# Window attention with graph experts on one core: another order of the first stage's side tasks, in 8 slots per image

## The reference, cut to what matters

```python
x = x + _L0_conv_ref(_ln_c(x), w_qkv, b_qkv, w_o, b_o)     # two window attentions
t = _to_tokens(x)
t = t + _L0_ffn_ref(_ln_t(t), ...)                          # graph attention, top 2 of 4 experts
```

## Time and profile before

| what | value |
|---|---|
| median of 3 runs | 7772.78 us |
| the profiled execution: its time | 7765.42 us |
| its span, first to last instruction | 7763.3 us |
| stage `attention` in it | 0 to about 1878 us |
| busy in the whole span: PE, DVE, ACT, POOL | 50%, 63%, 28%, 67% |

### The profile page before, as it was taken

The page is one execution under the profiler, slowest core; times in us unless marked ns, Lnnn a source line. Parts: engine busy times, 40 slices in busy tenths (PEclk is TensorE's granted clock), DMA queues, the critical chain, the costliest instruction groups (busy, mean ns, idle before and its releaser), DMA issues. The chain is left out here.

```text
span 7763.3 us, 91006 instructions
## 1 busy us (share of the span) xinstructions
PE 3878.5 (50%) x32088; PEld 2504.7 (32%) x32088; DVE 4875.5 (63%) x6373; ACT 2140.9 (28%) x4331; POOL 5177.2 (67%) x5802
## 2 busy tenths in 40 slices
PE   5889999996334334333433333343334334333347
PEld 3667676664122212212221222122122212211123
DVE  9999999997455445545554554455455445545578
ACT  4779888884111111111111111111111111111000
POOL 4443444434777777777777777777777777777674
PEclk8999999997666666666666666666666666666578
DMA  1222222223112111111211111111112111111188
GB/s 51 54 58 63 63 61 66 64 55 73 33 34 44 33 33 39 38 33 33 45 33 33 39 38 33 33 43 35 33 33 44 33 33 39 38 33 33 34 258 278
DMA packets 504189, 417.71 MB, mean 54 GB/s; under 512 B 161058, under 2 KB 400850, under 8 KB 503378
## 3 DMA queue, kind: packets, MB, share of 16 engines
q1 hardware_dynamic: 322562, 340.11, 13.8%
q0 software_dynamic: 181344, 73.74, 9.4%
HBM read 203.44 MB, written 176.45 MB: 49 GB/s over the span
## 5 line engine op out<-in xcount | busy, mean ns | idle before, releaser
L1646 POOL DMA_INDIRECT edge_G<-node_rows,edge_src x4352 | 4127.2, 948 | 1326.3 <-issue 1326.3
L1701 PE MATMUL edge_hbank<-edge_xt,edge_w 128*128 128x512 f32 x1024 | 718.4, 858 | 2754.8 <-ACT edge_hid L1671 2740.6
L1450 DVE TENSOR_TENSOR edge_oh<-edge_wbank,edge_dlf 128x3072 bf16<-128x3072 f32 x512 | 1682.9, 3350 | 57.1 <-PE edge_cbank L1726 41.6
L1407 DVE COPY edge_O<-edge_O 128x24 f32<-128x24 f32 x64 | 12.3, 192 | 2349.4 <-DMA edge_G<-node_rows,edge_src 2349.4
L1701 PEld LDWEIGHTS edge_hbank<-edge_xt,edge_w 128*128 128x128 f32 x1024 | 253.6, 274 | 3184.0 <-ACT edge_hid L1671 3032.5
L1681 ACT ACTIVATE edge_w<-edge_w 128x272 f32<-128x272 f32 x64 | 27.5, 429 | 4048.4 <-DVE edge_w L1421 4048.4
L1726 PE MATMUL edge_cbank<-edge_oh 128*128 128x256 bf16 x4096 | 803.3, 366 | 650.2 <-DVE edge_oh L1450 649.8
L1726 PEld LDWEIGHTS edge_cbank<-edge_oh 128*128 128x128 bf16 x4096 | 476.9, 125 | 952.8 <-DVE edge_oh L1450 815.3
L599 POOL TENSOR_TENSOR attn_att<-attn_oraw,attn_rsum 128x512 f32<-128x512 f32 (+1 forms) x136 | 169.7, 1248 | 827.4 <-DVE attn_rsum L1143 735.1
L1070 DVE TENSOR_TENSOR attn_keys<-attn_keys 128x1024 f32<-128x1024 f32 (+1 forms) x340 | 480.2, 1412 | 9.8
L1075 DVE TENSOR_TENSOR attn_keys<-attn_keys 128x1024 f32<-128x1024 f32 (+1 forms) x340 | 481.3, 1416 | 0.0
(11 more groups left out here) (281 smaller groups left out, 6556.6 us busy)
## 6 DMA issues: line engine op xcount, KB each, us to landing
edge_G<-node_rows,edge_src POOLq DMA_INDIRECT x4352, 2.4
expert_out<-edge_yo SPq DMA_DIRECT2D x64, 1024.0 KB, 4.3
comb_ye<-expert_out SPq DMA_DIRECT2D x32, 2048.0 KB, 13.7
state_rows<-edge_O SPq DMA_DIRECT2D x64, 816.0 KB
attn_km<-attn_kT SPq DMA_DIRECT2D x1024, 32.0 KB, 2.0
attn_xin<-in_x SPq DMA_DIRECT2D x32, 512.0 KB, 4.3
attn_x<-in_x POOLq DMA_DIRECT2D x64, 256.0 KB, 4.8
x_rows<-attn_x SPq DMA_DIRECT2D x32, 512.0 KB, 3.3
```

Of the source, the lines that this page charges most:

```text
L1450: dve.tensor_tensor(oh[:, r:r + WIDE, :, :].rearrange("p t k n -> p (t k) n"), iota.unsqueeze(1).to_broadcast([P, 3 * WIDE, P]), dlf[:, t: ...
L1646: pool.indirect_dma_start(G[b][:, t, :], None, node_rows, bass.IndirectOffsetOnAxis(ap=src[b][:, t:t + 1], axis=0)).then_inc(s_g[b][2 * t ...
L1701: pe.matmul(hbank[k % 2][:, :], w1[:, k // HB, (k % HB) * P:(k % HB + 1) * P], xt[b][:, :], start=True, stop=True).then_inc(s_l1, 1)
```

## The change

Four pairs of tasks move, and the sort's table follows. `Ao1`, `Bo1` go from slot 3 to slot 4. `Ao0`, `Bo0` go from slot 7 to slot 0 of the next step (lags 0 and 2 become 1 and 3). `CZ0`, `CZ1` go from slot 5 to slot 6, with POOL's DMAs behind them; the statistics of x2 on DVE and `deviation(1)` on POOL go from slot 7 to slot 0 of the next step. `CH0` goes from slot 6 to slot 5, ahead of `Bk0`; `Bq0` stays in slot 6, now behind the CZ tasks. `Bv0` goes from slot 0 to slot 7 of the step before (lag 2 becomes 1), and its wait is written for the new place. SP stores the turned tokens before x2. The table in `spare` gets eight new numbers.

```diff
-        SLOT_TASKS = [["Av0", "Bv0"],
+        SLOT_TASKS = [["Av0", "Ao0", "Bo0"],
                       ["Ak1", "Bk1", "Aq1"],
                       ["Bq1", "Av1", "Bv1"],
-                      ["FT0", "FT1", "Ao1", "Bo1"],
-                      ["Ak0", "Aq0"],
-                      ["Bk0", "CZ0", "CZ1"],
-                      ["Bq0", "CH0"],
-                      ["CT0", "CT1", "Ao0", "Bo0"]]
-        LAG = {"Av0": 0, "Bv0": 2, ...
+                      ["FT0", "FT1"],
+                      ["Ak0", "Aq0", "Ao1", "Bo1"],
+                      ["CH0", "Bk0"],
+                      ["CZ0", "CZ1", "Bq0"],
+                      ["CT0", "CT1", "Bv0"]]
+        LAG = {"Av0": 0, "Bv0": 1, ...
...
-               "Bk0": 1, "Bq0": 1, "CZ0": 3, "CZ1": 3, "Ao0": 0, "Bo0": 2, ...
+               "Bk0": 1, "Bq0": 1, "CZ0": 3, "CZ1": 3, "Ao0": 1, "Bo0": 3, ...
...
-            busy += (0.85, -0.1, 0.05, 0.2, 3.05, -0.5, 0.55, 2.4)[j]
+            busy += (2.65, 0.4, 0.05, 0.8, 2.55, -0.2, 0.1, 0.1)[j]
...
# SP: the store of x2 (CZ0) now stands behind the store of the turned tokens (CT0)
...
# POOL
-                    if j == 5 and active("CZ0", n):
+                    if j == 6 and active("CZ0", n):
                         add_residual(n - LAG["CZ0"])
-                    if j == 7 and active("CZ0", n):
-                        deviation(1, n - LAG["CZ0"])
+                    if j == 0 and active("CZ0", n - 1):
+                        deviation(1, n - 1 - LAG["CZ0"])
...
# ACT, values()
-                    act.wait_ge(s_pv, (n - 1) * PAIRS + 4 * h + 4)
+                    act.wait_ge(s_pv, (m - 1 + LAG[task[0]]) * PAIRS + 4 * h + 4)
...
# DVE
-                    if j == 7 and active("CZ0", n):
-                        m = n - LAG["CZ0"]
+                    if j == 0 and active("CZ0", n - 1):
+                        m = n - 1 - LAG["CZ0"]
                         dve.wait_ge(s_added, 32 * m + 32)
                         statistics(1, x2, range(TILES), m)
```

More of the change, by code:

```diff
@@ L361, in attention @@
         s_store = sem("s_store")
-        SLOT_TASKS = [["Av0", "Bv0"],
+        SLOT_TASKS = [["Av0", "Ao0", "Bo0"],
                       ["Ak1", "Bk1", "Aq1"],
                       ["Bq1", "Av1", "Bv1"],
-                      ["FT0", "FT1", "Ao1", "Bo1"],
-                      ["Ak0", "Aq0"],
-                      ["Bk0", "CZ0", "CZ1"],
-                      ["Bq0", "CH0"],
-                      ["CT0", "CT1", "Ao0", "Bo0"]]
-        LAG = {"Av0": 0, "Bv0": 2, "Ak1": 0, "Bk1": 2, "Aq1": 0, "Bq1": 2, "Av1": 0, "Bv1": 2,
+                      ["FT0", "FT1"],
[3 more added lines that the diff above has]
+                      ["CT0", "CT1", "Bv0"]]
+        LAG = {"Av0": 0, "Bv0": 1, "Ak1": 0, "Bk1": 2, "Aq1": 0, "Bq1": 2, "Av1": 0, "Bv1": 2,
                "FT0": -1, "FT1": -1, "Ao1": 1, "Bo1": 3, "Ak0": -1, "Aq0": -1, "CH0": 5,
-               "Bk0": 1, "Bq0": 1, "CZ0": 3, "CZ1": 3, "Ao0": 0, "Bo0": 2, "CT0": 4, "CT1": 4, "A": 0, "B": 2}
+               "Bk0": 1, "Bq0": 1, "CZ0": 3, "CZ1": 3, "Ao0": 1, "Bo0": 3, "CT0": 4, "CT1": 4, "A": 0, "B": 2}
         FIRST_STEP, LAST_STEP = -2, IMAGES + 5
@@ L503, in _ @@
                     sp.dma_start(node_rows[m].rearrange("(j p) d -> p j d", p=P), hrow[:, :, :]).then_inc(s_hst, 16)
-                if active("CZ0", n):
-                    m = n - LAG["CZ0"]
-                    sp.wait_ge(s_added, 32 * m + 32)
-                    sp.dma_start(x2_out[m].rearrange("(j p) d -> p j d", p=P), x2[:, :, :]).then_inc(s_x2st, 16)
                 if active("CT0", n):
@@ L512, in _ @@
                     sp.dma_start(tnT_out[m], tnT[:, :]).then_inc(s_tst, 16)
+                if active("CZ0", n):
+                    m = n - LAG["CZ0"]
+                    sp.wait_ge(s_added, 32 * m + 32)
+                    sp.dma_start(x2_out[m].rearrange("(j p) d -> p j d", p=P), x2[:, :, :]).then_inc(s_x2st, 16)
             for late in sorted(transfers):
```

## The result

The changed kernel takes 7726.53 us, the median of 6 runs that lie between 7721.21 and 7733.56. Runs of the kernel before on the same chips have the median 7775.12 us (7772.62 to 7777.56, 6 runs). The ratio is 0.994, with a 95% interval of 0.993 to 0.9951: 48.6 us less by the medians, 38 to 54 us by the interval. The profiled execution took 7724.29 us with a span of 7722.2.

The account below looks back on a forecast made before the run. DVE was taken to bound stage `attention`, its work fixed, so only idle time could go. Terms -33 - 12 + 3 + 2 + 2 = -38 us took the median from 7772.8 to 7735, range 7710 to 7765.

Parts of the forecast that it names:

- What bounds the stage: Stage `attention`: DVE bounds it, 95.5% busy from step 10 to 31; only its idle time, 114 us there, can go.
- The wait for x2, -33: Slots 6 to 0: DMAs land at 7.2 us, statistics come at 11.2, so of 36.1 us of waits 3 stay.
- The rival that the wait only moves: DMAs behind the product start later and land behind the statistics; 32 us come back, total 7767; chance 0.13.
- Late transposes, -12: `Ao`, `Bo` come a slot after POOL's product, so PE's wait for POOL goes; -12 us, bounds 0 and -17.8.
- DVE felt it as part of the 17.8 us: PE's wait for POOL mostly cost nothing; DVE felt it within its L927 score waits behind slots 7 and 3.
- Slot 4 and slots without sort operations, +3 and +2: PE's 6.8 us in slot 4 just covered by its lead, +3; heavier slots without sort operations in steps 27, 31, +2.
- The drain, +2: After the last scores the last x2 statistics come a slot later, but queues are empty; +2 us, bounds 0 and 8.
- unchanged within 5 us: Profile sign: DVE's busy time to 1881 us stays the same within 5 us.
- DVE's work is fixed: Score passes, statistics and sort operations stay and are only spread by the planner, so only DVE's idle time can go.
- PE as the bound in slots 4 to 6: Rival: PE's lead missing in slot 4, DVE idles 2.4 us in 30 images, +72 - 3, total 7804; chance 0.07.
- The key copies: Rival: copies late for slot 4, 0.7 us per image back, total 7756, chance 0.04; PE waiting there a sign of error.
- That all waits go: Rival: evenly loaded PE also ends the L932 score waits except steps 27 and 31; -64, less 3, total 7712; chance 0.12.

Follow-up runs that it names:

- x2 half: Kernel before with only CZ tasks, `CH0`, POOL's DMAs, x2 statistics, `deviation(1)`, SP's order and 2.2 us of the table moved; 7736.76 us, 0.9944; again 0.9947.
- only the statistics late: Kernel before with only the x2 statistics, `deviation(1)` and 2.2 us of the table moved to slot 0 of the next step; 7760.31 us, 0.998.
- second profile of the changed kernel: The changed kernel run once more with no edit, against the kernel before on the same chip; 7723.56 us, 0.9937.
- the drain reordered: Changed kernel, last steps only: last two products ahead of image 30's `deviation(1)`, last statistics a slot earlier, ACT's normalisation of image 30 a slot later; 7724.96 us, 0.9941.
- the DMAs ahead of the product: Changed kernel with POOL issuing the two x2 DMAs ahead of slot 6's product by the row sums instead of behind it; 7735.71 us, 0.9951.
- coarse table: Changed kernel with the old numbers in `spare`, except 2.2 us for the statistics moved from slot 7 to slot 0; 7755.43 us, 0.9964 to the kernel before.
- fine table alone: Kernel before with only the new numbers in `spare`, the statistics' 2.2 us left in slot 7, all tasks where they were; 7787.21 us, 1.0005.
- attended half: Kernel before with only the attended tasks moved to slots 4 and 0 and `Bv0` to slot 7; 7776.65 against 7783.36 us, 0.9991.
- only the DMAs late: Kernel before with only POOL's x2 DMAs moved to slot 6 behind the product, CZ in slot 5, statistics in slot 7; 7854.07 against 7777.4 us, 1.0101.

## Why the prediction was right, point by point

**What bounds the stage.** Right: DVE. But the slots got shorter by two things where the prediction had one, by DVE's idle time (-42.8) and by its busy time (-12.3).

**The wait for x2, -33.** Measured -31.4 in the slots (34.4 to 3.0). The chain was worked out as 7.2 us for the landing against 11.2 for the statistics. The same step of the changed kernel:

```profile
969.29 0.34 DVE L1143 RECIPROCAL attn_rsum<-attn_oraw 128x32 f32<-128x32 f32 x1
969.78 1.06 POOL L599 TENSOR_TENSOR attn_att<-attn_oraw,attn_rsum 128x512 f32<-128x512 f32 x1 [0.35 <-DVE attn_rsum L1143]
970.78 2.69 POOL L583 DMA_DIRECT2D attn_x<-in_x  x2
980.34 1.58 DVE L1059 BATCH_NORM_STATS2 attn_st<-attn_x 128x6 f32<-128x128 f32 x8
```

The statistics come 11.05 us after the reciprocal. The issues end as forecast, but the landing takes longer:

```profile
DMA to landing us min/median/max: 4.4/5.7/8.0
```

The median is 5.7 us instead of 4.8. The second landing is then at about 970.78 + 1.35 + 5.7 = 977.8, and the margin is 2.5 us, not 4. With landings of up to 8.0 us it isn't enough everywhere: three waits are left, 1.8, 0.7 and 0.5 us, in steps 10, 11 and 19. The rival that the wait only moves was nearer than its 11.2 against 7.2 said, and the two kernels that leave the statistics in slot 7 behind late DMAs show it in full (127.3 and 110.4 us of waits).

**Late transposes, -12.** Measured 17.8 to 5.8 us under L927, exactly this, and in part by luck. It isn't the gain of moving the transposes: moved alone they gave 0.9991, and the x2 half, which leaves them where they were, got 8.0 of the 12.0 us, since its product was short again. The step "DVE felt it as part of the 17.8 us" was right as a row and incomplete as a cause, for more of the same lateness was hidden under the wait for x2, as the kernel with only the statistics late showed (32.9 us).

**Slot 4 and slots without sort operations, +3 and +2.** The waits under L932 for the scores of slot 5 went from 4.4 us in 7 to 6.1 in 7, so +1.7. Step 27 has 4.5 and 4.4 us of waits for the scores of slots 6 and 7 (8.9 where "some 7.5" was forecast, from terms that add up to 7.8; 4.51 before), step 31 4.1 for those of slots 3 and 4 instead of 5.8 for those of slots 2 and 3: +2.7 together. The sum under L932 is 0.7 up, as other steps lost some. The cover of PE's lead in slot 4 held with the new table and not with the coarse one.

**The drain, +2.** Measured +7.1, near the bound of 8, and +4.9 in the second profile of the changed kernel. "The queues are empty then and the data set the time" was wrong here. The last product of the kernel before, and then the drain of the changed kernel:

```profile
1843.95 1.41 POOL L599 TENSOR_TENSOR attn_att<-attn_oraw,attn_rsum 128x256 f32<-128x256 f32 x1 [1.39 <-DVE attn_rsum L1143]
```

```profile
1785.70 0.38 POOL L562 TENSOR_TENSOR attn_nw<-attn_st 128x8 f32<-128x8 f32 x1 [1.52 <-DVE attn_st L1059]
...
1792.20 0.24 DVE L1143 RECIPROCAL attn_rsum<-attn_oraw 128x16 f32<-128x16 f32 x1
...
1794.81 1.18 POOL L576 TENSOR_TENSOR attn_nw<-attn_nw 128x8 f32<-128x8 f32 x1
1795.96 1.59 POOL L599 TENSOR_TENSOR attn_att<-attn_oraw,attn_rsum 128x256 f32<-128x256 f32 x1
...
1797.70 1.09 PE L865 MATMUL attn_misc<-attn_ident,attn_att 128*128 128x128 f32 x4 [7.11 <-POOL attn_att L599]
...
1805.51 1.37 POOL L583 DMA_DIRECT2D attn_x<-in_x  x1 [7.95 <-ACT attn_x L696]
...
1821.85 0.20 POOL L576 TENSOR_TENSOR attn_nw<-attn_nw 128x8 f32<-128x8 f32 x1
```

The last reciprocal is there at 1792.20, but POOL is in `deviation(1)` of image 30 until 1796, and the last product starts 3.75 us after its reciprocal. In the kernel before POOL waited 1.39 us for this reciprocal and started 0.38 us after it, so the queue cost nothing. Followed along this chain, the 7.1 us are 0.4 to the reciprocal, 3.4 to the product, 1.8 from there to the issue of the last DMA, and 1.6 in its landing (1807.23 to 1814.73, against 5.9 us before); from the last statistics to `edges` both kernels take 19.3. The first three are -0.4, 3.4 and 1.6 in the second profile, and the landing 0.3, so the landing is mostly chance. The three sort operations that moved here are not on this chain. `deviation(1)` itself is slow: 10.3 us for image 30, with sort operations of 128x1024 beside its end, against 5.6 us for image 31; its last instruction takes 1.18 us there and 0.20 here. The kernel with the drain reordered takes the product ahead of it, and its drain is 2.7 to 4.9 us shorter.

**What the sum had not.** Shorter DVE operations, and three fewer in the slots. DVE is busy 9.2 us less over slots and drain, where the prediction had "unchanged within 5 us"; 6.9 of these are the sort's plain operations (6.3 those of the shape above) and 1.7 the statistics. The step that failed is "DVE's work is fixed", that is, the time of its operations taken as fixed: the prediction looked at POOL's product, whose 1.06 us did hold in all 120 products of 128x512, and left out that the DVE operation beside it had been stretched as well, 2.69 us in the earlier trace rows where others take 2.29. The Trainium skill, SBUF — State Buffer, section Who interferes with whom, says that a DVE instruction with two SBUF inputs contends with a GpSimd instruction that reads SBUF. The traces agree, and the cost is on both sides: with the DMAs ahead of the product DVE's stretch is 14.1 us. Of the 12.3 us that DVE is busy less in the slots, 3.7 are the three sort operations that the new table places behind the start of the last slot, where the chain above, and not DVE, sets the time. The prediction has no term for them.

The forecast summed to -38: x2 -33, transposes -12, slots +5, drain +2. Measured by the same terms: -31.4, -12.0, +0.7, +7.1, and -12.3 for DVE's busy time in the slots: -47.9. The errors are +1.6, 0, -4.3, +5.1 and -12.3, together -9.9: the drain's error hid a part of the other two.

**The rivals.** PE as the bound in slots 4 to 6 did not come, but the coarse table brought 20.9 us of waits for the scores of slot 5, where this rival had 72. The key copies: PE did wait for them ahead of slot 4, which the prediction had as a sign of being wrong, but by 5.1 us in nine steps. Eight times DVE didn't wait behind it; in step 31 it waited 2.9 us behind a wait of PE of 1.0. That is far from the 0.7 us per image of this rival, whose own numbers (3.15 + 2 + 11.29 + 2.0 = 18.4 us against 18.5) didn't give the 0.7 either. That all waits go did not come either, since steps 27 and 31 keep theirs.

## What to carry to other kernels

One wait of an engine can hide another that stands behind it: take the first away, and the hidden one shows in its place, so cost a change with each of them taken away in turn. A moved producer and its moved consumer are one edit: here one alone cost 77 us and the other gave 17, and both, with the projection moved along, gave 47 and 38 us in two measurements. When a tensor operation on POOL runs beside a long operation on DVE with two SBUF inputs, count the stretch on both engines; beside an operation that reads PSUM there was none here.

## What the runs showed of the hardware

POOL's product of 128x512 takes 1.06 us beside a maximum or a subtraction on DVE that reads PSUM. Beside DVE's 128x2048 minimum or maximum with two SBUF inputs it takes up to 4.1 us, and that operation 2.69 to 3.03 us instead of 2.29. Beside the 128x1024 form it takes up to 3.03 us, and that operation, for one, 2.06 instead of 1.22. POOL's last operation of a deviation (L576, 128x8), from 700 us on in the kernels before and after, takes 1.06 to 1.28 us in all 29 cases that overlap a sort operation and 0.20 in the 52 that don't. POOL's pair of DMA issues takes 2.69 us beside a sort operation as beside others.

The same 64 DMAs that add x land after 4.8 us (median) in the kernel before, 4.9 with only the statistics late and 5.1 with the fine table alone; after 5.3 with the attended half, with only the DMAs late and with the DMAs ahead of the product, and after 5.7 and 5.9 in the changed kernel and its x2 half. What in the other traffic delays them was not tried.
